# A decoder block on one core: per-engine call lists written out in place of a table of ticks

## The chip, the core and the metric

One core of a Trainium2 chip runs the whole program in one launch. The metric is the device time of one execution in microseconds (us). The kernel before has a median of 279.81 us over 3 runs (279.69 to 280.71). One further execution was profiled; it took 280.03 us, of which 278.30 us lie between its first and last instruction (the span). All positions below are us from the start of that span.

## The reference, cut to what matters

Three pre-LayerNorm blocks, each added to x (8 batches of 128 tokens, 256 wide):

```python
def _L0_attn_ref(x, Wq, Wk, Wv, Wo):        # 16 heads of 16
    scores = jnp.einsum('bthd,bshd->bhts', q, k)
    scores = scores * jnp.tril(jnp.ones((T, T)))      # masked scores are 0, not -inf
    attn = jax.nn.softmax(scores / T ** 0.5, axis=-1)
    out = jnp.einsum('bhts,bshd->bthd', attn, v).reshape(B, T, H * Dh)
    return out @ Wo
def _L0_xattn_ref(k, v, q, ssm_kernel, D, head_dim):   # k = v = ctx_2048, 16 heads of 8 x 8 products
    kv = jnp.einsum('bhil,bhjl->bijhl', k_, v_)
    y = irfft(rfft(kv, 2L) * rfft(ssm_kernel, 2L))[..., :L]     # a causal convolution over 256
    out = jnp.einsum('bijhl,bhil->bjhl', y + kv * D, q_)
def _L0_ffn_ref(x, ...):                    # 4-bit codes times block scales, 256 -> 2048 -> 256
    inter = gelu(x @ Wg.T) * (x @ Wu.T)
    return inter @ Wd.T
x = x + _L0_attn_ref(_layernorm(x), ...)
x = x + _L0_xattn_ref(ctx_2048, ctx_2048, _layernorm(x), ssm_kernel, D, 8)
x = x + _L0_ffn_ref(_layernorm(x), ...)
```

## The kernel before

The program is written engine by engine: one in-order instruction list each for TensorE, VectorE, ScalarE, GpSimd and SyncE, joined by semaphores. An instruction that waits holds everything behind it in its engine's list. There are three parts in time.

Up to about 28.7 us: x is normalised and transposed, split into a high and a low half-precision part, and projected to q, k and v. q and k go through a scratch tensor in DRAM (L347, L355) to be packed into the tile QK, in two groups of four batches.

Then the middle, until unit 8 of the MLP. `convolve(h, lc)` (L1024 on) does the causal convolution of one head in three matmuls; each result is copied out of psum by `conv_out` on ScalarE, and the factors are formed by `products(h)` on VectorE and on GpSimd in a ring of four. The first CONV_EARLY = 9 heads use the four psum banks 2 to 5 and run ahead of everything else, the others use banks 6 and 7. For each batch b the attention then goes: `scores(b, p)` on TensorE; `pair_max` (L816) and `max_pieces` (L832 to L836) on VectorE; a transpose of the maxima (L1186); `mT` (L685) on ScalarE; two small DMAs into rows of QK, issued by SyncE (`max_rows`, L363); `scores_t(b, p)` (L1092), which waits for those rows; exp (`probs`, L596); `attend` (L1108); `pv_out`; a transpose (L1209) and the sum over later tokens (L1213); `normalise` (L842 to L851) on VectorE; a transpose of the heads (L1219); the output projection with the residual (L1163, L1165); X is copied back (L712). Then LayerNorm 2 (statistics on VectorE L725, eps on ScalarE L643, power on GpSimd L403, apply on ScalarE L651), the transposed query (L1196), `conv_products` on GpSimd (L476 and L479, one call per half), their sum (`sum_slots`, L886) on VectorE, the add (L1177, L1179), LayerNorm 3 and the transposed MLP input (L1203), split by ScalarE (L698) and VectorE (L925).

The MLP is 32 units: `gate_and_up(u)` (L980, 12 matmuls), gelu (L635) and `act_hi` (L625) on ScalarE, `gate_up` (L894) on VectorE, `act_lo` (L500) on GpSimd, `down(u)` (L1150, 12 matmuls). Units 0 to 7 need only batches 0 to 3 and run between the last batches of the middle; unit 8 is the first that needs all eight. The 4-bit weights are decoded per step j: a DMA of codes and scales (`load_codes`, L301 to L306), four integer operations on VectorE (`codes_split`, `codes_join`, L859 to L871), two products on GpSimd (`decode_scale`, L492), the high part on ScalarE (`w_hi_step`, L618) and the low part on VectorE (`w_lo`, L876). ScalarE also issues the code loads of steps 1 to 3 behind its w_hi_step.

The order of the middle comes from a table: every kind of call has a tick (T_SCORES = 0, T_ST = 4, T_QT = 10, T_YT = 15 and so on), a batch every two ticks, UNIT_TICKS for the eight early units, DECODE for the four early steps. Each engine's part has one loop `for t in range(TICKS)` that runs through the kinds in one fixed order in every tick:

```python
(T_SCORES, T_SPLIT, T_MPT, T_ST, T_ATT, T_PVOUT, T_TOK, T_NORM, T_OT, T_PROJ, T_LN2, T_RSTD2, T_APPLY2,
 T_QT, T_MIX, T_MIX2, T_SUM, T_SUM2, T_RT, T_LN3, T_RSTD3, T_APPLY3, T_YT) = (
    0, 1, 3, 4, 5, 6, 7, 7, 8, 9, 8, 9, 9, 10, 11, 12, 12, 12, 13, 13, 14, 15, 15)
CONV_EARLY = 9
CONV_RATE = 2
UNIT_TICKS = (22, 23, 24, 24, 25, 26, 28, 29)
DECODE = (1, 5, 19, 23)
```

Psum banks 6 and 7 are handed from call to call: `take(n, reader, count)` makes TensorE wait for the reader of the call that used the bank last in its list, so a new order also makes new pairs.

Behind the middle stands a plain loop over units 8 to 31 on each engine, then the residual add and the output DMAs.

Of the kernel before, what the change touches and what calls it, by code (L numbers as in the profile page):

```python
# [37 lines left out]

def build(nc, x_d, ctx_d, wqkv_d, wo_d, ker_d, skip_d, gu_scale_d, down_scale_d, codes_d, out_d):  # L50
# [4 lines left out]
    with ctx:  # L55
# [9 lines left out]

# [37 lines left out]
        def bits2(j):  # L103
# [62 lines left out]

# [49 lines left out]

        (T_SCORES, T_SPLIT, T_MPT, T_ST, T_ATT, T_PVOUT, T_TOK, T_NORM, T_OT, T_PROJ, T_LN2, T_RSTD2, T_APPLY2,  # L230
         T_QT, T_MIX, T_MIX2, T_SUM, T_SUM2, T_RT, T_LN3, T_RSTD3, T_APPLY3, T_YT) = (
            0, 1, 3, 4, 5, 6, 7, 7, 8, 9, 8, 9, 9, 10, 11, 12, 12, 12, 13, 13, 14, 15, 15)
# [10 lines left out]
        TICKS = max(2 * (B - 1) + T_YT, UNIT_TICKS[-1],  # L243
                    DECODE[EARLY - 1] + 3) + 1

# [5 lines left out]
        def early_units(t):  # L251

            return [u for u, tick in enumerate(UNIT_TICKS) if tick == t]

        def early_decode(t, at):

            return [j for j in range(EARLY) if DECODE[j] + at == t]

# [4 lines left out]

        def batch(t, at):

            b, r = divmod(t - at, 2)
            return [b] if r == 0 and 0 <= b < B else []

        def pair_of_groups(t, at):

            n = t - at
            return [divmod(n, 2)] if 0 <= n < 2 * B else []

        def group(t, at):

            return [(b, 2 * p + par) for b, p in pair_of_groups(t, at) for par in range(2)]

        def conv_heads(t):

            return [h for h in range(CONV_EARLY + CONV_RATE * t, CONV_EARLY + CONV_RATE * (t + 1)) if h < H]  # L280

# [94 lines left out]
        def _(pool):  # L376
# [124 lines left out]

            for h in range(KVR, CONV_EARLY + CONV_RATE):
                products(h)
            for t in range(TICKS):
                for b in batch(t, T_MIX2):
                    conv_products(b, 1)
                for b in batch(t, T_RSTD3):
                    pool.wait_ge(s_veps[2], b + 1)
                    rstds(2, b, 1)
                for j in early_decode(t, 2):  # L510
                    decode_scale(j, 1)
                for h in conv_heads(t + 1):
                    if h >= KVR:
                        products(h)
                for b in batch(t, T_MIX):
                    conv_products(b, 0)
                for b in batch(t, T_RSTD2):
                    pool.wait_ge(s_veps[1], b + 1)
                    rstds(1, b, 1)
                for j in early_decode(t, 1):  # L520
                    decode_scale(j, 0)
                for u in early_units(t):
                    if u >= 1:
                        act_lo(u - 1)
# [7 lines left out]
        def _(sc):  # L532
# [94 lines left out]
            def unit(u):  # L627
# [9 lines left out]
                if u >= 1:  # L637
                    act_hi(u - 1)
# [15 lines left out]
            for h in range(CONV_EARLY):  # L654
                for lc in range(2):
                    conv_out(h, lc)
            for t in range(TICKS):
                for b in batch(t, T_QT):
                    sc.wait_ge(s_qt, b + 1)
                    if b >= 2:  # L660
                        sc.wait_ge(s_z, 4 * (b - 2) + 4)
                    s_.activation(view(qx[:, b % 2], [[16, 2 * H], [1, HD]], 4),
# [10 lines left out]
                for b in batch(t, T_RSTD3):  # L673
                    ln_eps(2, b)
# [615 lines left out]
```

## Time and profile before

| what | value |
|---|---|
| median of 3 runs | 279.81 us (279.69 to 280.71) |
| profiled execution | 280.03 us, span 278.30 us |
| TensorE busy | 250.9 us, 90% of the span |
| VectorE, ScalarE, GpSimd busy | 162.5, 129.9, 149.3 us |
| mean granted TensorE clock | 0.972 |
| first convolution matmul | 28.66 us |
| first gate matmul of unit 0 | 138.96 us |
| first gate matmul of unit 8 | 177.50 us |
| last down matmul ends | 272.60 us |

In the rows PE is TensorE's matmuls, PEld its weight loads, DVE VectorE, ACT ScalarE, POOL GpSimd, SP SyncE; a q behind the name is the engine's own sequencer or the DMAs that it issues. L and a number is a line of the kernel. Busy shares average over parts with different limits, so the stages are to be read singly.

### The profile page before, as it was taken

To read this page: it belongs to the slowest core of one execution; us is meant where nothing else is said; L and a number is where in the kernel's file an instruction comes from. 1 tells how busy PE (TensorE), PEld (TensorE's weight loads), DVE (VectorE), ACT (ScalarE), POOL (GpSimd) and SP (SyncE) were. 2 spreads that over 40 slices of the span, in tenths; PEclk is the share of its full clock that TensorE was granted. 3 is DMA by queue.
4 is the path that set the end of the run, shared out by engine and by line. 5 is a ranking of instruction groups with operands and counts; after the bars stand their busy time and mean duration, and the time that the engine had idled before them with its cause. 6 is when DMAs were issued, how large, how long until landed. Compare 5 with 4: busy or idle time off the path is not lost.

```text
span 278.3 us, 5004 instructions
## 1 busy us (share of the span) xinstructions
PE 250.9 (90%) x1872; PEld 161.9 (58%) x1872; DVE 162.5 (58%) x280; ACT 129.9 (47%) x281; POOL 149.3 (54%) x172
## 2 busy tenths in 40 slices
PE   7999999965999887895598998999999999999993
PEld 7765775533665655673454655556665566556662
DVE  2888523989786999668658364251725446131114
ACT  2454665545466666764555254331435243432230
POOL 3278464413116596759988995228354554723330
PEclk9999999999799999978979999999999999999998
DMA  6998969130300000000420030000303000000004
GB/s 200 389 318 199 181 224 173 30 114 4 117 1 4 2 1 6 1 2 0 124 102 2 0 115 0 1 4 0 113 2 113 3 2 0 0 2 0 0 2 151
DMA packets 15104, 18.81 MB, mean 68 GB/s; under 512 B 1448, under 2 KB 12776, under 8 KB 15080
## 3 DMA queue, kind: packets, MB, share of 16 engines
q1 hardware_dynamic: 13832, 16.13, 21.4%
q10 hardware_dynamic: 1248, 2.36, 2.7%
q8 instruction: 15, 0.25, 0.4%
q14 instruction: 9, 0.07, 0.1%
HBM read 15.21 MB, written 3.15 MB: 66 GB/s over the span
## 4 chain that ended last, share of the span: by engine, by line
PE 56%; DVE 5%; POOL 4%; issue 3%; ACT 2%; DVEq 0%; POOLq 0%; ACTq 0%
PE bank L980 30%; PE bank L1150 15%; PE bank L1165 2%; PE bank L1163 2%; POOL w L492 1%; PE bank L1177 1%; DVE o_sb L851 1%; POOL arena L476 1%; PE bank L1179 1%; PE bank L1108 1%; DVE XN L946 1%; ACT XN L651 1%; POOL rstd L403 1%; POOL arena L479 1%; PE bank L1203 1%
## 5 line engine op out<-in xcount | busy, mean ns | idle before, releaser
L500 POOL TENSOR_TENSOR QK<-QK 128x512 f16<-128x512 f32 x31 | 35.9, 1160 | 56.0 <-ACT QK L625 56.0
L894 DVE SCALAR_TENSOR_TENSOR QK<-bank,QK 128x512 f32<-128x512 f32 x32 | 22.0, 689 | 61.2 <-PE bank L980 61.2
L635 ACT ACTIVATE QK<-bank 128x512 f32<-128x512 f32 x32 | 19.1, 597 | 70.5 <-PE bank L980 70.3
L980 PE MATMUL bank<-xTh,Wa 128*128 128x512 f16 x128 | 41.9, 389 | 0.0
L980 PE MATMUL bank<-xTh,Wb 128*128 128x512 f16 x128 | 40.7, 379 | 0.0
L476 POOL TENSOR_TENSOR arena<-Ys,qx 128x640 f32<-128x640 f32 x16 | 25.1, 1568 | 2.0 <-ACT qx L665 2.0
L980 PE MATMUL bank<-xTl,Wa 128*128 128x512 f16 x64 | 25.0, 391 | 0.0
L980 PE MATMUL bank<-xTl,Wb 128*128 128x512 f16 x64 | 24.3, 379 | 0.0
L816 DVE TENSOR_REDUCE mx<-bank 128x8 f32<-128x1024 f32 x16 | 19.4, 1212 | 7.7 <-PE bank L1073 7.6
L1150 PE MATMUL bank<-Wa,QK 128*128 128x256 f16 x192 | 23.6, 273 | 0.0
L403 POOL TENSOR_TENSOR rstd<-veps,nhalf 128x1 f32<-128x1 f32 x16 | 9.6, 597 | 25.6 <-ACT veps L643 25.6
L1150 PE MATMUL bank<-Wb,QK 128*128 128x256 f16 x192 | 23.3, 273 | 0.0
L1150 PEld LDWEIGHTS bank<-Wa,QK 128*128 128x128 f16 x192 | 18.8, 98 | 5.6 <-POOL QK L500 0.2
L1150 PEld LDWEIGHTS bank<-Wb,QK 128*128 128x128 f16 x192 | 18.7, 98 | 5.3
L492 POOL TENSOR_TENSOR w<-arena 128x768 f32<-128x768 f16 x12 | 21.7, 1813 | 0.0
L725 DVE BATCH_NORM_STATS2 stats<-X 128x6 f32<-128x256 f32 x24 | 10.0, 417 | 19.0 <-ACT X L712 10.6
L980 PEld LDWEIGHTS bank<-xTh,Wa 128*128 128x128 f16 x128 | 12.8, 100 | 14.0 <-issue 1.3
L886 DVE TENSOR_REDUCE R<-arena 128x128 f32<-128x1024 f32 x16 | 18.9, 1207 | 2.7 <-POOL arena L479 2.7
L625 ACT ACTIVATE QK<-QK 128x512 f16<-128x512 f32 x32 | 19.9, 622 | 1.0 <-DVE QK L894 1.0
L980 PEld LDWEIGHTS bank<-xTh,Wb 128*128 128x128 f16 x128 | 12.5, 98 | 13.4
L446 POOL TENSOR_TENSOR arena<-arena 128x320 f32<-128x320 f32 x16 | 13.7, 865 | 12.0 <-PE bank L1038 12.0
L479 POOL TENSOR_TENSOR arena<-Ys,qx 128x384 f32<-128x384 f32 x16 | 20.1, 1256 | 0.0
(145 smaller groups left out, 509.8 us busy)
## 6 DMA issues: line engine op xcount, KB each, us to landing
arena<-in_ker SPq DMA_DIRECT2D x2, 1024.0 KB, 12.0
QK<-qk_scratch SPq DMA_DIRECT2D x8, 256.0 KB, 5.9
arena<-in_ctx SPq DMA_DIRECT2D x2, 768.0 KB, 7.8
qk_scratch<-Wa SPq DMA_DIRECT2D x12, 128.0 KB, 3.4
arena<-in_codes SPq DMA_DIRECT2D x4, 384.0 KB
QK<-qk_scratch SPq DMA_DIRECT2D x8, 128.0 KB, 5.8
arena<-in_gu_scale SPq DMA_DIRECT2D x4, 256.0 KB
out<-XN SPq DMA_DIRECT2D x4, 256.0 KB, 2.4
```

Source lines behind the costliest of these rows:

```text
L446: g_.tensor_tensor(view(KV[:, h % KVR, m, :], [[40, B], [8, NPAIR], [1, HD]]), view(a, [[12 * H, B], [0, NPAIR], [1, HD]]), view(a, [[12 * ...
L476: g_.tensor_tensor(view(Z[:, r], [[64, H], [1, NPAIR], [NSLOT, HD]], rows), view(Ys[:, 0, 0], [every, [DIAG, NPAIR], [1, HD]], convolved), ...
L479: g_.tensor_tensor(view(Z[:, r], [[64, H], [1, 3], [NSLOT, HD]], rows + NPAIR), view(Ys[:, 0, 0], [every, [DIAG - 1, 3], [1, HD]], convolv ...
L492: g_.tensor_tensor(W32[:, nib, :], view(bits(j).bitcast(F16), [[2, 768]], nib), scales(j), ALU.mult).then_inc(s_w32, 1)
L500: g_.tensor_tensor(il[:, u % IR], val[:, u % VR], ih[:, u % IR], ALU.subtract).then_inc(s_il, 1)
L625: s_.activation(ih[:, u % IR], val[:, u % VR], ACT.Copy).then_inc(s_ih, 1)
L635: s_.activation(val[:, u % VR], bank[2 * (u % 2)][:, :], ACT.Gelu_apprx_tanh, scale=1.0 / W_GAIN).then_inc(s_gel, 1)
L816: v_.tensor_reduce(mx[:, b % 2, 8 * p:8 * p + 8], psum[:, 0:2, :].rearrange("p g (h t) -> p (g h) t", h=4), AX.X, ALU.max).then_inc(s_max, 1)
L886: v_.tensor_reduce(R[:, b % 2, H * half:H * half + H], view(Z[:, b % 2], [[NSLOT, H * HD], [1, NSLOT]], 1024 * half), AX.X, ALU.add).then_ ...
L894: v_.scalar_tensor_tensor(out=val[:, u % VR], in0=bank[2 * (u % 2) + 1][:, :], scalar=UP_SCALE, in1=val[:, u % VR], op0=ALU.mult, op1=ALU. ...
L980: ins = mmul(out, a(c), w(c), start=(n == 0), stop=(n == 3 * len(chunks) - 1))
L1150: last = mmul(out, a[:, u % IR, t], w[j % RW][:, nib, 512:768], start=((j, nib) == (0, 0) and tt % 2 == 0 and n == 0), stop=((j, nib) == ( ...
```

## The change

The tick table, its helper functions and the five loops over ticks are gone. Each engine's part now has small named functions (one kind of call each, with the waits that the loop body had) and a list of single calls written out one under the other. Every operation stays on its engine, with its operands and its waits; the lists order them anew, in no regular pattern. CONV_EARLY is 13, so heads 0 to 12 use psum banks 2 to 5 and the first `scores_t` waits for the copies of 13 heads. The convolutions are no longer ahead of everything: `row_scores(0, 0)` stands behind head 3. VectorE's products(h), formerly ahead of the ticks up to head 10, are mixed into the list. ScalarE's `unit(u)`, which did gelu(u) and act_hi(u - 1) together, is split into two calls. SyncE's list is as before. The loop over units 8 to 31 is as before. The diff, cut to its core (renamed helpers keep their bodies):

```diff
-        (T_SCORES, T_SPLIT, T_MPT, T_ST, T_ATT, T_PVOUT, T_TOK, T_NORM, T_OT, T_PROJ, T_LN2, T_RSTD2, T_APPLY2,
...
-        CONV_EARLY = 9
-        CONV_RATE = 2
+        CONV_EARLY = 13
-        UNIT_TICKS = (22, 23, 24, 24, 25, 26, 28, 29)
-        EARLY = len(UNIT_TICKS) // 2
-        DECODE = (1, 5, 19, 23)
+        EARLY = 4
...
 GpSimd
+            products(8)
+            decode_scale(0, 0)
+            products(9)
+            products(10)
+            decode_scale(0, 1)
...
+            decode_scale(1, 0)
+            decode_scale(1, 1)
+            decode_scale(2, 0)
+            rstd_cross(0)
+            decode_scale(2, 1)
+            conv_products(0, 0)
+            conv_products(0, 1)
+            rstd_cross(1)
+            rstd_cross(2)
...
+            conv_products(5, 1)
+            rstd_ffn(4)
+            decode_scale(3, 0)
+            rstd_cross(7)
+            decode_scale(3, 1)
+            act_lo(0)
+            rstd_ffn(5)
+            act_lo(1)
+            conv_products(6, 0)
+            conv_products(6, 1)
+            conv_products(7, 0)
+            act_lo(2)
+            conv_products(7, 1)
...
 ScalarE
+            def decode_hi(j):
+                w_hi_step(j)
+                if j + 1 < EARLY:
+                    load_codes(sc, j + 1)
...
+            conv_out(8, 0)
+            decode_hi(0)
+            conv_out(8, 1)
+            conv_out(9, 0)
+            take_max(0)
...
+            pv_out(0)
+            take_max(1)
+            decode_hi(1)
+            probs(1, 0)
...
 VectorE
+            products(4)
+            products(5)
+            products(6)
+            decode_codes(0)
+            pair_max(0, 0)
+            products(7)
...
+            ffn_lo(1)
+            w_lo(2)
+            sum_slots(3, 1)
+            ffn_lo(2)
+            normalise(6)
+            stats_cross(5)
+            stats_ffn(3)
+            sum_slots(4, 0)
+            sum_slots(4, 1)
+            stats_cross(6)
+            normalise(7)
...
 TensorE
-            for h in range(CONV_EARLY):
-                for lc in range(2):
-                    convolve(h, lc)
...
+            convolve(3, 1)
+            row_scores(0, 0)
+            convolve(4, 0)
...
+            convolve(6, 1)
+            row_scores(0, 1)
+            convolve(7, 0)
...
+            row_scores(2, 1)
+            key_scores(0, 0)
+            convolve(14, 0)
+            convolve(14, 1)
+            key_scores(0, 1)
+            convolve(15, 0)
+            attend(0, 0)
+            row_scores(3, 0)
+            convolve(15, 1)
...
+            attend(7, 3)
+            project_out(5)
+            add_cross(3)
+            turn_heads(6)
+            turn_values(7)
+            project_out(6)
+            turn_ffn(3)
+            turn_query(5)
+            add_cross(4)
+            turn_heads(7)
+            gate_and_up(0)
+            turn_query(6)
+            project_out(7)
+            gate_and_up(1)
+            turn_ffn(4)
+            add_cross(5)
+            gate_and_up(2)
+            gate_and_up(3)
+            down(0)
+            down(1)
+            turn_ffn(5)
+            turn_query(7)
+            gate_and_up(4)
+            gate_and_up(5)
+            add_cross(6)
+            gate_and_up(6)
+            down(2)
+            gate_and_up(7)
+            turn_ffn(6)
+            add_cross(7)
+            down(3)
+            down(4)
+            down(5)
+            turn_ffn(7)
             for u in range(2 * EARLY, UNITS):
                 gate_and_up(u)
                 down(u - 2)
```

## Rows read from the trace of the kernel before

**Rows 1.** The page's chain of work that ended last: share of the span by engine.
```profile
PE 56%; DVE 5%; POOL 4%; issue 3%; ACT 2%; DVEq 0%; POOLq 0%; ACTq 0%
```
**Rows 2.** Busy time by stage: stretch, length, busy per engine (count), clock, DMA share, GB/s.
```profile
28.66:43.29 14.63, 14.63 (x57) 10.07 (x56) 4.69 (x11) 9.95 (x35) 7.62 (x8) 1.00 0.89 207
43.29:83.80 40.51, 33.42 (x383) 21.30 (x382) 33.35 (x51) 21.93 (x55) 11.42 (x11) 0.96 0.31 68
83.80:139.00 55.20, 43.61 (x467) 30.57 (x468) 43.53 (x80) 33.53 (x77) 41.92 (x45) 0.94 0.07 18
139.00:177.50 38.50, 35.99 (x205) 21.78 (x202) 21.16 (x31) 18.80 (x40) 30.35 (x29) 0.96 0.12 40
177.50:272.60 95.10, 95.10 (x592) 57.62 (x590) 35.85 (x46) 32.89 (x53) 41.98 (x32) 1.00 0.06 18
```
**Rows 3.** The chain in order of time, late loop: start, us, what.
```profile
263.46 2.59 PE bank L980 x12
266.05 1.31 PE bank L1150 x12
```
**Rows 4.** The same chain in the middle, around the calls of three batches.
```profile
89.64 1.38 DVE o_sb L851
...
91.15 0.41 PE bank L1219 x2
91.56 0.56 PE bank L1108 x16
92.12 0.67 PE bank L1163 x2
92.79 0.86 PE bank L1165 x4
93.66 0.33 PE bank L1056 x4
93.98 0.23 PE bank L1073 x8
...
94.49 0.67 PE bank L1177 x2
95.16 0.44 PE bank L1179 x4
95.61 0.16 PE bank L1186
...
96.32 0.59 PE bank L1209 x4
96.91 0.47 PE bank L1213 x2
```
**Rows 5.** TensorE's waits from 28 to 178: who for whom, total, times, longest.
```profile
PE bank L1196 <- ACT XN L651: 5.9, 6, 2.7
PE bank L1056 <- DMA QK<-mT: 4.2, 5, 2.3
```
**Rows 6.** Single lines: ns min/median/max, first and last start; L816 from the page's groups.
```profile
L816 DVE TENSOR_REDUCE mx<-bank 128x8 f32<-128x1024 f32 x16 | 19.4, 1212 | 7.7 <-PE bank L1073 7.6
...
L851 DVE TENSOR_TENSOR o_sb<-num,rec x8: 424/1126/1720, 74.8 to 137.1; 128x256 f32<-128x256 f32 x8
...
L476 POOL TENSOR_TENSOR arena<-Ys,qx x16: 1554/1570/1577, 83.8 to 162.9; 128x640 f32<-128x640 f32 x16
...
L479 POOL TENSOR_TENSOR arena<-Ys,qx x16: 999/1024/2512, 85.3 to 164.4; 128x384 f32<-128x384 f32 x16
```
**Rows 7.** GpSimd in order of time beside the first row of Rows 4.
```profile
89.15 1.58 POOL L476 TENSOR_TENSOR arena<-Ys,qx 128x640 f32<-128x640 f32 x1
```
**Rows 8.** SyncE's issues (codes; packing of group 1) and VectorE's first decode, by time.
```profile
28.13 0.60 SPq L301 DMA_DIRECT2D XN<-in_codes  x1
...
39.67 5.10 SPq L355 DMA_DIRECT2D QK<-qk_scratch  x8
...
50.28 0.55 DVE L859 TENSOR_SCALAR xTl<-XN 128x768 int32<-128x768 int32 x1
```

More of the change, by code:

```diff
@@ L500, in act_lo, with rstd_cross @@
                 g_.tensor_tensor(il[:, u % IR], val[:, u % VR], ih[:, u % IR], ALU.subtract).then_inc(s_il, 1)
[L502 to L524, printed above, removed]
+            def rstd_cross(b):
+                pool.wait_ge(s_veps[1], b + 1)
+                rstds(1, b, 1)
@@ new lines, in _ @@
+            take_out(7)
+            ln_apply(2, 4)
+            gate_gelu(1)
+            ln_eps(1, 7)
+            take_ffn(4)
+            act_hi(0)
+            take_cross(5)
+            act_hi(1)
+            gate_gelu(2)
+            ln_apply(1, 7)
+            ln_eps(2, 5)
+            act_hi(2)
+            gate_gelu(3)
+            ln_apply(2, 5)
+            decode_hi(3)
+            act_hi(3)
+            take_query(7)
+            take_ffn(5)
+            gate_gelu(4)
+            act_hi(4)
@@ new lines, in turn_heads, with turn_max @@
+            def turn_heads(b):
+                take(7, s_ott, b + 1)
+                pe.wait_ge(s_och, 4 * b + 4)
+                for c in range(2):
+                    last = t_.transpose(bank[7][:, P * c:P * c + P], o_sb[:, b % 2, P * c:P * c + P],
+                                        ident[:, :])
+                last.then_inc(s_ot, 1)
+            def turn_max(b):
+                take(7, s_mt, b + 1)
+                pe.wait_ge(s_mch, b + 1)
+                mmul(bank[7][0:2 * H, 0:P], mp[:, b % 2, :], identh[:, :], start=True, stop=True).then_inc(s_mpt, 1)
@@ new lines, in _ @@
+            project_out(3)
+            key_scores(4, 1)
+            row_scores(7, 0)
+            attend(4, 0)
+            turn_max(6)
+            attend(4, 1)
+            key_scores(5, 0)
+            attend(4, 2)
+            attend(4, 3)
+            key_scores(5, 1)
+            turn_values(4)
+            attend(5, 0)
+            key_scores(6, 0)
+            row_scores(7, 1)
+            turn_ffn(0)
+            attend(5, 1)
+            add_cross(1)
+            turn_heads(4)
+            key_scores(6, 1)
@@ new lines, in _ @@
+            attend(5, 2)
+            project_out(4)
+            turn_query(3)
+            attend(5, 3)
+            attend(6, 0)
+            attend(6, 1)
+            add_cross(2)
+            attend(6, 2)
+            attend(6, 3)
+            turn_max(7)
+            turn_values(5)
+            turn_ffn(1)
+            turn_query(4)
+            key_scores(7, 0)
+            turn_values(6)
+            turn_heads(5)
+            key_scores(7, 1)
+            turn_ffn(2)
+            attend(7, 0)
```

608 lines of the change are left out of this document (423 added, 185 removed).

## The prediction

> **What bounds the kernel now.** I read the chain of work that ended last first. Its shares by engine [rows 1] give TensorE 56%; followed in time, the chain is one unbroken run of TensorE from 173.76 us on: each further unit of the MLP is 2.59 us of gate and up matmuls and 1.31 us of down matmuls [rows 3], with nothing between. From 177.50 to 272.60 TensorE is busy 95.10 of 95.10 us at full granted clock (last row of [rows 2]). That loop (units 8 to 31 and the last two downs) isn't touched by the change, and what follows it (residual add, output) isn't either. So the whole question is when unit 8 starts; everything behind it is a constant. The other end of the stretch is fixed too: up to 28.66 us (LayerNorm 1, projections) no call list is touched. What the change can move is the stretch from 28.66 to 177.50, 148.8 us.
>
> In that stretch I read the busy time by stage [rows 2]. TensorE is idle 0 us, then 40.51 - 33.42 = 7.1, then 55.20 - 43.61 = 11.6, then 38.50 - 35.99 = 2.5: 21.2 us in all. The granted clock is below 1 in the last three: 0.96, 0.94 and 0.96 of stretches of 40.5, 55.2 and 38.5 us, which is 1.6 + 3.3 + 1.5 = 6.4 us of TensorE time lost at the lower level of 1.2 GHz. In the same rows VectorE has 33.35 of 40.51 and 43.53 of 55.20 us: in these two it is as loaded as TensorE, which matters below. The waits say what ended the idle time [rows 5]: TensorE stood for LayerNorm's result from ScalarE (5.9 us in 6 waits) and for the row maxima that travel by DMA (4.2 us in 5 waits). These are latencies of a chain that goes TensorE, VectorE, ScalarE, GpSimd and back, cut by in-order queues. A better order can hide them.
>
> **The work that stays.** No operation is added, removed or given to another engine; only the order in each queue changes. So I count what TensorE must issue between 28.66 and unit 8. Convolutions: nine heads fill the 14.63 us of the first stretch [rows 2], so sixteen take 26.0. From the chain's pieces [rows 4]: row scores 0.33 + 0.23 = 0.56, the key scores the same, 32 in all, 17.6 (I take 0.55); attention with V 0.56 per two groups, 16 times, 9.0; output projection 0.67 + 0.86 = 1.53, 8 times, 12.2; adding the cross block 0.67 + 0.44 where TensorE isn't packed and less where it is, I take 0.95, 7.6; turning the values 0.59 + 0.47 = 1.06, 8.5; turning the heads 0.41, 3.3, and the query and MLP input about the same, 6.1; the maxima 0.16, 1.3. Eight gate and up at 2.59 and six down at 1.31 [rows 3]: 20.7 + 7.9. The sum is 120.2 us. Check: 120.2 + 21.2 idle + 6.4 clock = 147.8 of 148.8; 1.0 us is left over and I carry it.
>
> **What is moved.** I followed the four new call lists by hand beside each other, each call at the duration of its rows, each wait as written.
>
> Convolutions. Nine heads ran ahead of any attention, then two per tick; now row scores (0,0) come after four heads, and thirteen heads use the four banks of psum 2 to 5. Row scores need the packed scratch DMAs of group 0. SyncE has issued them by about 28.1, just before the codes [rows 8], and I take them as landed by 35.1, when head 3 ends (TensorE waits at most 1 us if not). VectorE decodes the codes of step 0 ahead of the row maximum (0,0), after products(6), and not at 50.28 [rows 8] but from about 37.5, when I take the codes as landed: four operations, 2.9 us. Behind that wait on VectorE's queue stand the maximum (0,0), products(7) and, through them, TensorE's row scores (0,1) and head 7. I get 1.1 us of TensorE idle there. ScalarE's decode_hi(0), with its wait for both decode_scale(0) and its three DMA issues, now stands ahead of conv_out(8,1); behind it waits convolve(10,1), which needs that bank. It costs nothing as long as head 10 is reached after about 48.6, which is so in my walk by about 0.5 us. In return, at 60 to 61 us two more row scores, both key scores of batch 0 and an attention group are already issued. Thirteen heads in banks 2 to 5 make the first key scores wait for conv_out(12,1), about 54.7, which is 1.5 us ahead of its need. Row scores (3,0), issued at 65.1 before, end at 60.4.
>
> Attention. Per batch TensorE has some 8 us and VectorE has four reduces of 1.21 [rows 6] (maxima, and sums over as many elements), and by my reading of its shorter calls some 3.7 more, about 8.5. My walk puts single waits of 0.3 to 1.2 us: for the mT rows before key scores (1,0), which now come after the ScalarE decode_hi(1) with its DMA issues; for exp before (1,1); for XN and take_query around 87 to 91; for take_ffn and the last mT rows at 109 to 111. The first product of the cross block on GpSimd starts at about 79.3 and not 83.80 (first start of L476 [rows 6]), as project_out(0) comes at 69.6. The last attend ends near 115.7; before, it ended near 130.9.
>
> Tail. After the last attend TensorE still has about 42 us of work, and the chain of the last batch (values, normalise, heads, projection, statistics, query, 5.2 us of products on GpSimd, sum, statistics, MLP input, low part) is about 21.6 us long. So units 0 to 7 cover it if they start early. The first, gate_and_up(0), starts at 125.5 in my walk (139.0 before), the last products end on GpSimd near 150.2 (164.4 + 2.5 = 166.9 before [rows 6]). At the end stands a wait the old order did not have: turn_ffn(7) is TensorE's last call before unit 8, and ffn_lo(7) follows it; 0.9 to 1.2 us (before, unit 7 and down(5) lay between). GpSimd's act_lo and decode_scale(3) are moved past the cross products; SyncE's list is as it was, and its code loads for steps 4 to 7 depend on earlier events than before.
>
> **The sum.** In the walk unit 8 starts at 161.6, 132.9 us after 28.66; the calls as the walk costs them (projections at 1.46, the shorter of two patterns) are 118.9 of these, so its waits are 14.0 us. The walk has no low clock. The clock fell before behind the thin stretch at 60 to 70 and again between 118 and 144; fewer idle gaps should leave about half, 3.0 us (bounds 0 and 6.4). So 120.2 + 1.0 + 14.0 + 3.0 = 138.2 us in place of 148.8: -10.6 us. On the profiled execution's 280.03 us (its span 278.30, rest 1.73) this is 269.4 us. That execution is 0.2 above the median of the runs, 279.81, which changes nothing.
>
> **A rule weighed.** normalise's last operation takes between 0.42 and 1.72 us [rows 6]. One of 1.38 starts at 89.64 [rows 4] while a product of GpSimd runs from 89.15 to 90.73 [rows 7], and ends 0.3 us behind it, the time that a short one needs. The Trainium skill (SBUF — State Buffer, "Who interferes with whom") says that a VectorE instruction with two SBUF inputs contends with a GpSimd instruction that reads SBUF and fully blocks if it comes second; the trace agrees. It speaks against this change, as a denser GpSimd blocks more VectorE work. In rows of this case: my walk has normalise at 1.6 us, unblocked. Before, the median was 1.13, some 0.7 us of loss in each; if all eight are blocked at the longest, 1.72 - 0.42 = 1.3 us each, it is 10.4 us of VectorE. I expect most of it beside TensorE's other work; rival F is the case that it isn't.
>
> **Rivals.**
> A, forecast: 269.4.
> B, GpSimd's own queue keeps its pace. Its sixteen cross products took from 83.8 to 166.9, 83.1 us, for 16 x (1.57 + 1.02) = 41 us of work at the medians [rows 6]. If blocked VectorE work and ScalarE's queue stretch them again to 83.1 from 79.3, they end at 162.4 and unit 8 comes 10.6 us later as before, at 173.0: -4.5, 275.5. For it: VectorE is as full as TensorE up to 139. Against: the gaps were waits for veps and qx, which now come earlier.
> C, denser than my walk: no low clock and 11 us of waits: 120.2 + 1.0 + 11 = 132.2, -16.6, 263.4. For it: TensorE's work allows it, and GpSimd's floor (79.3 + 41, about 20 for rstds, decodes and low parts between, and 6.5 for the chain behind the last product) is 147. Against: I have left every blocked operation out.
> D, slower: the codes of step 0 land late. decode_codes(0) holds VectorE's queue from 35.6 and TensorE's heads 7 to 15 behind it. Issued at 28.13 while the DMA engines are full (share 0.89 to 43.3 [rows 2]), they are only known to be there at 50.28. If they land then, all behind slips by 50.28 - 37.5 = 12.8 us: -10.6 + 12.8 = +2.2, 282.2. It decides from a landing at about 48. Against: SyncE's wait for scratch writes issued after the codes ended at 39.67 [rows 8].
> E, nothing: the new waits eat the old ones, 279.8.
> F, every o_sb operation (L851) is blocked behind a GpSimd product and all of it is on the path: -10.6 + 10.4 = -0.2 us, 279.8 too. For it: VectorE's load up to 139; against: TensorE has other calls queued before most turn_heads.
>
> **How the numbers follow.** A 0.52, B 0.17, C 0.15, D 0.10, E 0.03, F 0.03. Predicted 269.4. The range leaves D, E and F out and the far ends of C and B: 263.0 to 277.0. Beyond 0.5% (1.4 us, what a measurement of this kernel can tell from none) faster: A, B, C, 0.84; within: E and F, 0.06; slower: 0.10.
>
> **What would show it.** Right: unit 8 at 165 to 169 with the loop behind it at 95.1 us as before; TensorE idle between 28.66 and there 13 to 16 us; last attend near 116; the first gate matmul near 126 to 130; L476 first at about 79. Wrong: VectorE's L859 waiting for a DMA past 42 with TensorE idle behind it (D); L479's last end past 160 and L851's mean above 1.3 us (B); a granted clock under 0.9 over the units 0 to 7, which would double their 28.6 us in part.

## The result

Twenty runs of the changed kernel have a median of 282.8 us (279.9 to 285.43), twenty of the kernel before beside them 279.94: the ratio is 1.0088, with a 95% interval of 1.0058 to 1.0119. It is slower by 0.9%, where 3.7% faster was forecast (269.4), and lies above the range. The profiled execution of the changed kernel took 281.73 us, span 280.0, mean granted clock 0.966.

| | before | forecast | after |
|---|---|---|---|
| first GpSimd cross product | 83.80 | 79.3 | 93.8 |
| last attend ends | 130.9 | 115.7 | 132.6 |
| unit 0 starts | 138.96 | 125.5 | 143.21 |
| unit 8 starts | 177.50 | 166.9 | 179.20 |
| TensorE idle from 28.66 to unit 8 | 21.2 | 15.0 | 22.6 |
| lost to the lower clock there | 6.4 | 3.0 | 8.4 |

The busy time by stage of the changed kernel, columns as in [rows 2]: the convolutions, the first batches, the middle up to unit 0, units 0 to 7, the late loop.

```profile
28.66:43.29 14.63, 12.58 (x64) 8.46 (x64) 6.75 (x13) 8.34 (x29) 5.63 (x6) 1.00 0.91 210
43.29:83.80 40.51, 33.02 (x285) 21.06 (x283) 31.50 (x44) 18.73 (x51) 14.06 (x12) 0.87 0.33 71
83.80:143.21 59.41, 47.29 (x565) 33.35 (x560) 51.34 (x85) 37.75 (x84) 39.79 (x45) 0.96 0.09 29
143.21:179.20 35.99, 35.05 (x205) 21.71 (x204) 23.43 (x33) 19.57 (x41) 30.76 (x30) 0.98 0.08 23
179.20:274.30 95.10, 95.10 (x590) 57.62 (x591) 35.84 (x45) 32.89 (x53) 42.04 (x32) 1.00 0.06 18
```

The late loop is the constant it was taken for: 95.10 us, TensorE full, clock 1.00. The idle time is 150.54 us less 127.95 of busy TensorE, 22.6 us; only 0.9 of it is left in units 0 to 7, as forecast. The clock column costs 40.51 x 0.13 + 59.41 x 0.04 + 35.99 x 0.02 = 8.4 us. VectorE has 51.34 of the 59.41 us up to unit 0. TensorE's waits from 28 to 180 us, us in total, times, longest:

```profile
PE bank L1268 <- DVE mx L943: 5.1, 4, 2.5
PE bank L1268 <- DMA QK<-mT: 3.6, 2, 3.0
PE bank L1399 <- DVE o_sb L978: 2.8, 2, 2.4
...
PE bank L1196 <- DVE xTl L1037: 0.9, 1, 0.9
```

TensorE's 5.9 us of waits for LayerNorm's result ahead of turn_query [rows 5] are gone, as meant; 1.2 us of such waits are left ahead of turn_ffn. In their place TensorE waits four times, 5.1 us, for the row maximum (L943), which VectorE's own queue holds up (before it was one wait of 2.5 us), and one wait for the maxima that travel by DMA is now 3.0 us.

Following the chain of work that ended last through the front shows how the first of these goes (start us, us, what; L986 and L900 from VectorE's order of time first):

```profile
39.18 0.56 DVE L986 TENSOR_SCALAR xTl<-XN 128x768 int32<-128x768 int32 x1 [4.92 <-DMA XN<-in_down_scale]
...
42.84 5.04 DVE L900 TENSOR_TENSOR arena<-arena 128x320 f32<-128x320 f32 x4
```
```profile
41.71 1.22 DVE mx L943
42.93 0.76 DVE arena L900
...
43.95 3.94 DVE arena L900 x3
47.89 1.14 DVE mx L943
49.03 0.05 issue
49.08 0.39 PE bank L1268 x4
```

VectorE stood 4.92 us for the codes of step 0, decoded them, and only at 41.71 took the maximum of row scores that had long been there. products(7) to (10) behind it took 5.04 us for four where a single one takes 0.49, beside GpSimd's reads; the longest of the sixteen products operations took 2.09 us here and 1.03 in the kernel before. Row scores (0,1) waited 1.99 us, (1,0) 2.52 us, and from 49 to 52 us TensorE's matmuls ran at the lower clock level.

The second place in the chain is at key scores (1,0):

```profile
70.76 0.60 SPq L299
71.36 0.04 issue
71.40 3.89 DMA QK<-mT
75.30 0.05 issue
75.34 0.40 PE bank L1268 x4
```

ScalarE's order of time at that place says what else was under way:

```profile
70.47 0.27 ACT L657 ACTIVATE mT<-bank 32x128 f16<-32x128 f32 x1
70.56 0.34 ACTq L237 DMA_DIRECT2D arena<-in_codes  x1
```

The rows' two transfers of 4 KB were handed over by SyncE from 70.76 us on, 0.2 us behind the first of the three loads (384 of 768 KB) with which decode_hi(1) fetches the codes of step 2; the other two followed at 70.92 and 71.57. From its hand-over to its landing the second transfer took 3.89 us. Key scores (1,0) themselves still ran at the upper level; behind a further wait of 1.12 us for exp, from 77.1 to 83.3 us, TensorE ran at the lower one.

### The profile page after: what moved, and what is told of

Its sections match the earlier page's. It is cut to its first block, busy times and chain, and to the rows that moved or that the text cites. A ratio compares the mean times of both kernels' runs of the same rounds, so it can differ in the third digit from the quotient of the medians.

```text
span 280.0 us, 5004 instructions
## 1 busy us (share of the span) xinstructions
PE 250.8 (90%) x1872; PEld 162.0 (58%) x1872; DVE 172.8 (62%) x280; ACT 130.1 (46%) x281; POOL 148.3 (53%) x172
## 4 chain that ended last, share of the span: by engine, by line
PE 75%; DVE 15%; DMA 3%; issue 2%; ACT 2%; POOL 1%; SPq 1%; DVEq 0%; POOLq 0%
PE bank L1196 36%; PE bank L1362 15%; PE bank L1268 3%; PE bank L1252 3%; PE bank L1254 3%; DVE mx L943 3%; PE bank L1250 2%; DVE arena L900 2%; PE bank L1436 2%; DVE o_sb L978 2%; DMA X<-in_x 2%; PE bank L1320 1%; DMA QK<-mT 1%; PE bank L1387 1%; PE bank L1304 1%
## 5 line engine op out<-in xcount | busy, mean ns | idle before, releaser
L1196 PE MATMUL bank<-xTh,Wa 128*128 128x512 f16 x128 | 41.2, 385 | 0.9 <-DVE xTl L1037 0.9
L412 POOL TENSOR_TENSOR arena<-Ys,qx 128x640 f32<-128x640 f32 x16 | 26.9, 1684 | 5.0 <-ACT qx L669 5.0
L558 ACT ACTIVATE Ys<-bank 128x320 f32<-128x320 f32 x32 | 14.5, 454 | 18.1 <-PE bank L1254 13.1
L943 DVE TENSOR_REDUCE mx<-bank 128x8 f32<-128x1024 f32 x16 | 19.5, 1216 | 3.2 <-PE bank L1285 3.2
L578 ACT ACTIVATE PT<-bank 128x1024 f32<-128x1024 f32 x16 | 16.4, 1027 | 10.3 <-PE bank L1304 10.0
L339 POOL TENSOR_TENSOR rstd<-veps,nhalf 128x1 f32<-128x1 f32 x16 | 8.8, 551 | 19.6 <-ACT veps L623 19.4
```

The source lines that it names most:

```text
L412: g_.tensor_tensor(view(Z[:, r], [[64, H], [1, NPAIR], [NSLOT, HD]], rows), view(Ys[:, 0, 0], [every, [DIAG, NPAIR], [1, HD]], convolved), ...
L558: s_.activation(view(Ys[:, h, lc], [[YROW, B], [DIAG, NPAIR], [1, HD]]), conv_bank(h, lc)[:, 0:320].rearrange("p (b d m) -> p b d m", b=B, ...
L578: s_.activation(PT[:, 2 * (n % 2):2 * (n % 2) + 2].rearrange("p g h t -> p g (h t)"), psum[:, 2:4, :], ACT.Exp, scale=SCALE).then_inc(s_ex ...
L943: v_.tensor_reduce(mx[:, b % 2, 8 * p:8 * p + 8], psum[:, 0:2, :].rearrange("p g (h t) -> p (g h) t", h=4), AX.X, ALU.max).then_inc(s_max, 1)
L1196: ins = mmul(out, a(c), w(c), start=(n == 0), stop=(n == 3 * len(chunks) - 1))
```

## The experiments

Ratios are to the kernel before, in the same set of runs. The changed kernel stands at 1.0088 (1.0058 to 1.0119) from its own set, so a difference to it carries both intervals. Positions are from one profiled execution of each kernel. They scatter: in the changed kernel, x1 and y1 below, whose calls are the same up to there, turn_max(0) starts at 54.69, 52.27 and 55.44 us.

**Which half of the order.** Two kernels take one half of the order from each side.

```diff
 g1: per engine
-(new list)
+(the calls of the old ticks 0 to 3, nine heads early), then the rest as in the new list
 g2: per engine
-(new list)
+(those same calls in the new order, thirteen heads early), then the rest as in the old list
```

> The changed kernel, but every engine first runs the calls of the old ticks 0 to 3 in the old order (nine heads ahead, CONV_EARLY 9, decode of step 0 late), then the rest in the new order. Theory FRONT (the loss is made in the first stretch: new row scores (1,0) came at 49.1 where my walk had 44.6, key scores (1,0) at 75.3 against 65.9): the rest of the new order is good, unit 8 starts near 170 to 173, 273 to 276 us. Theory PORTS (VectorE and GpSimd block each other more wherever the new order packs them): the middle keeps its loss, unit 8 at 177 to 180, 279 to 283 us.

> The reverse: the calls of the old ticks 0 to 3 in the new order (CONV_EARLY 13, row scores between the heads, step 0 decoded early), then all the rest in the old order. FRONT: as bad as or worse than the changed kernel, 283 to 287 us, since the front costs some 3 to 5 us and the old rest gains nothing. PORTS: near the kernel before, 279 to 282 us.

Measured: 1.0155 (1.0121 to 1.0189) and 1.014 (1.0057 to 1.0222). Both are slower than the kernel before, and neither is better than the changed one. g1 (284.04 us) lies above what either theory gave it, g2 (285.39) where FRONT put it. With the old front TensorE lost nothing up to 60 us (30.65 of 31.34 us busy, clock 1.00, as before), but from 60 to 100 the clock was 0.79. Neither half is the culprit by itself. I took that as a sign that the loss is in single places, which the runs below test.

**GpSimd's reads.** In both orders (p1 the new one, p2 the old), GpSimd's scale products and convolution products are replaced by memsets of the same tiles.

```diff
-g_.tensor_tensor(W32[:, nib, :], view(bits(j)...), scales(j), ALU.mult)
+own(g_.memset(W32[:, nib, :], 0.001))
+g_.memset(W32[:, nib, :], 0.001)
...
```

> The changed kernel with GpSimd's decode_scale and conv_products replaced by memsets of the same tiles and about the same length (two of 768 elements; two of 1024 and two of 512), so that GpSimd reads no SBUF in them: weights and cross products are constants, the output is not the reference's. PORTS: VectorE's busy time falls from 172.8 to about 155, o_sb is 0.42 us eight times, the products of head 7 to 10 take 2 us and not 5.0, unit 8 starts at 168 to 172, 271 to 275 us. If ports don't matter: VectorE's blocked operations overlap other waits and the time stays 280 to 283 us.

> The kernel before with the same replacement (the order written as lists, which is the old order call by call). PORTS: it gains less than the changed kernel does, 2 to 5 us, 275 to 278 us, so that the new order would be the faster one by some 3 us without the blocking. If it gains as much as the new order does, the blocking costs both alike and does not explain the difference.

Measured: new order 0.9898 (0.9825 to 0.9971), old order 0.9759 (0.9687 to 0.9832). By ratios that is 1.9% off the new and 2.4% off the old; the intervals do not tell these two apart. The new order gained less than the 271 to 275 us that PORTS gave it (279.22). GpSimd itself is about as busy with the memsets, 144.7 us in place of 148.3. VectorE's o_sb operation (its group over 28.66 to 180 us: line, shapes, count, busy us, mean ns) in the changed kernel, then with the memsets:

```profile
L978 DVE TENSOR_TENSOR o_sb<-num,rec 128x256 f32<-128x256 f32 x8 | 8.4, 1048 | 0.3
```
```profile
L976 DVE TENSOR_TENSOR o_sb<-num,rec 128x256 f32<-128x256 f32 x8 | 3.4, 429 | 0.3
```

products(7) to (10) take 2.74 us with the memsets in place of 5.04. So the blocking is real and worth some 5 us, but the old order pays it too. It explains a part of the forecast's miss, not why the new order is slower than the old.

**The load and the rows.** Two calls are moved; then each alone.

```diff
 ScalarE (x1, y1)
 take_max(1)
+take_max(2)
 decode_hi(1)
 probs(1, 0)
-take_max(2)
 VectorE (x1, y2)
-w_lo(1)
 pair_max(4, 0)
+w_lo(1)
```

> The new lists with two calls moved: on ScalarE take_max(2) stands directly behind take_max(1), so that the transfer of its rows is handed over before the 768 KB load of weight codes that decode_hi(1) sends off; on VectorE w_lo(1) stands behind pair_max(4,0). Theory QUEUE (key_scores(1,0) waited 3.03 us for rows that landed 3.89 us after their issue, beside the code load): it begins about 1.4 us earlier or more against the rows' issue, the half clock of 77 to 83 us goes, and the kernel is 3 to 4 us faster than the changed one (about 279). Theory ORDER (the slip is spread over every place where VectorE is late, no one load makes it): the end moves by under 1 us.

> One half of the two-call edit alone: ScalarE's take_max(2) directly behind take_max(1), so that the transfer of its rows is handed over before the code load of decode_hi(1) is sent off. Two calls moved gave a ratio of 0.9927 where the changed kernel has 1.0088, and key_scores(1,0) then waited 0.88 us for rows where it had waited 3.03. Theory QUEUE (the rows behind the 768 KB load are the cause): this edit alone brings most of it, ratio .993 to .997, rows landing within 2.3 us of their issue, and the half clock of 77 to 83 us is gone. Theory W_LO (the 1.75 us of w_lo(1) ahead of pair_max(4,0) on VectorE are what counts): this edit alone leaves 1.003 or more.

> The other half alone: VectorE's w_lo(1) behind pair_max(4,0). Theory QUEUE: no more than 1 us faster than the changed kernel, ratio 1.004 to 1.009, the rows of key_scores(1,0) still land 3.5 us or more after their issue. Theory W_LO: ratio .993 to .999.

Measured: both 0.9927 (0.9888 to 0.9967); ScalarE's call alone 0.9924 (0.9885 to 0.9963); VectorE's alone 1.0067 (1.0004 to 1.0131). The one call on ScalarE turns 0.9% slower into 0.8% faster, 4.6 us, and the other does nothing that can be told. The chain in the kernel with that one call moved:

```profile
72.15 1.75 DMA QK<-mT
```

The same transfer takes 1.75 us where it took 3.89, key scores (1,0) start 2.44 us after the hand-over (4.58 in the changed kernel), and the clock over 60 to 100 us is 0.96 in place of 0.87. Theory QUEUE stands. The load is not absent in this kernel: it is handed over at 72.59 us, 0.44 us behind this transfer. The edit also hands over the rows of batch 2 earlier, at 72.81 and not 77.20, but key scores (2,0) waited for nothing in either kernel.

**The same in the old order (w3).**

```diff
 ScalarE, kernel before
+decode_hi(1)
 take_max(2)
 probs(1, 1)
-decode_hi(1)
```

> The kernel before with one call moved on ScalarE: decode_hi(1), which sends off the 768 KB load of the codes of step 2, directly ahead of take_max(2), whose rows key_scores(2,0) needs; it stood two calls behind. Theory QUEUE (rows handed over right behind a code load land 1.5 us or more later, in whatever order of calls): the rows of batch 2 land 3.5 us or more after their issue, the time goes up by 1 to 4 us, ratio 1.004 to 1.014. Theory NEW ORDER ONLY (the old order has its rows two calls ahead of use and hides it): ratio within .003 of 1.

Measured: 1.0052 (1.0007 to 1.0098). The rows of batch 2 were handed over at 74.27 us and key scores (2,0) started at 78.09, 3.82 us later, after a wait of 1.43 us that the kernel before does not have there. So the place of this call matters in the old order too, and the old one loses about 1.5 us by it. This run does not show that the transfer alone is the reason. take_max(2) now also stands behind w_hi_step and the load's issue on ScalarE: its operand was there at 72.4 us and it ran at 73.98, so the rows were handed over some 1.6 us late before any byte of them moved. That alone covers the wait of 1.43 us; the slower way from hand-over to start (3.82 us, 2.44 in y1) would cover 1.38. The clean evidence for QUEUE is y1, where take_max(1), which hands over the rows of batch 1, kept its place.

**The decode earlier or later.** In the first kernel the decode of steps 0 to 2 stands as late as before on all engines; in the second, one call moved as above, w_lo(1) as in x1, and only step 0 later.

```diff
 VectorE (y3)
-decode_codes(0)
 pair_max(0, 0)
 ...
 max_pieces(0)
+decode_codes(0)
 ...
 products(15)
+w_lo(0)
 ScalarE (y3)
 conv_out(13, 1)
+decode_hi(0)
```

> The new lists, but the weight decode of steps 0 to 2 (codes, scale products, high and low halves, with the code loads that they send off) stands as late among the other calls as in the kernel before. Theory EARLY DECODE (some 9 us of decode put ahead of the first batches' maxima and of conv products on VectorE and ScalarE is what made row_scores(0,1), (1,0) and key_scores(1,0) wait, and each wait was followed by a stretch at half clock): the waits of 1.99 and 2.52 us at 41 to 49 us fall under 1 us each, unit 0 starts 4 to 6 us earlier than 143.2, and the end comes at 276 to 278. Theory ORDER (VectorE is the bound from 100 us on wherever the decode stands): the decode comes back later, unit 0 stays within 1.5 us of 143.2.

> The two calls moved, and the decode of step 0 moved later by itself: its codes on VectorE behind max_pieces(0) (they stood ahead of pair_max(0,0)), the low half behind products(15), its two scale products on GpSimd behind products(12) and (14), the high half on ScalarE behind conv_out(13,1). Steps 1 and 2 stay early. With all three late the third turn_max began 6 us earlier than in the changed kernel and unit 0 8 us later. Theory FRONT WAIT (the 4.92 us that VectorE waits for the codes of step 0 and the 3.6 us of scale products beside products(7) to (10) are lost for good): unit 0 at 132 to 134 against 136.6 with two calls moved, ratio about .98. Theory SHIFT (what step 0's decode does not cost at 36 to 48 us it costs at 50 to 60, where VectorE has as much to do; and the later load of the next codes makes step 1 late): ratio within .005 of .9927, unit 0 136 to 138.

Measured: 1.0315 (1.0248 to 1.0382) and 1.0116 (0.9994 to 1.0238). Both misses for the theories that made the early decode guilty. With all three late, turn_max(0) came at 48.40 us in place of 54.69, and unit 0 at 151.39 in place of 143.21: more was lost behind the front than it gained. In the second, VectorE's w_lo(0) waited 4.75 us for a high half that stood far back on ScalarE, so that kernel carries a fault of its own and says little of step 0. To have all three late is worse; the best place of each was open.

**Ahead of the codes.** Only two VectorE calls are taken out from behind the wait for the codes, with ScalarE's call moved as well and without.

```diff
 VectorE (v1; w2 with take_max(2) moved too)
+pair_max(0, 0)
+products(7)
 decode_codes(0)
-pair_max(0, 0)
-products(7)
```

> The changed kernel with take_max(2) behind take_max(1), and on VectorE pair_max(0,0) and products(7) ahead of decode_codes(0): VectorE stood 4.9 to 5.6 us waiting for the codes of step 0, which land at 39.2 to 39.9 us, while the maxima of row_scores(0,0), ready at 36.6 us, were queued behind it. Nothing else moves. Theory FRONT WAIT: row_scores(0,1) begins 1.5 to 2 us earlier than 42.98, and half or more of that arrives at unit 0: ratio .985 to .989 (one call moved gave .9924). Theory SHIFT (VectorE's work behind the codes begins when they land in either order, so pair_max(0,1) and row_scores(1,0) come no earlier): ratio .990 to .995.

> The changed kernel with one edit: on VectorE pair_max(0,0) and products(7) ahead of decode_codes(0); ScalarE's calls as in the changed kernel, so the rows of key_scores(1,0) still follow the code load. With both edits the ratio was 0.9858 and with the other alone 0.9924, in two sets, and their intervals touch. Theory FRONT WAIT (VectorE's wait for the codes is on the path by itself): ratio 1.000 to 1.004 where the changed kernel had 1.0088, row_scores(0,1) at 41.5 or earlier, unit 0 some 2 us earlier. Theory CHANCE (the difference of the two sets is scatter): 1.006 to 1.010.

Measured: with both 0.9858 (0.977 to 0.9947); alone 0.9959 (0.9928 to 0.999). Alone it is worth 1.3%, 3.6 us, more than its theory gave it (1.000 to 1.004). VectorE's first decode in it, and the transfer of the rows, which still follow the load:

```profile
38.39 0.56 DVE L986 TENSOR_SCALAR xTl<-XN 128x768 int32<-128x768 int32 x1 [0.91 <-DMA XN<-in_down_scale]
```
```profile
68.68 4.23 DMA QK<-mT
```

VectorE now waits 0.91 us for the codes and not 4.92, and TensorE's clock over 28.66 to 60 us is 1.00 in place of 0.95. Row scores (0,1) start at 40.79 without a wait (42.98 in the changed kernel), (1,0) at 45.54 in place of 49.08, turn_max(0) at 49.52 in place of 54.69. These positions flatter the edit: w2, with the same front, has turn_max(0) at 52.25 and a clock of 0.95 over 28.66 to 60, as without the edit. The ratio is the safer measure. A wait of 1.78 us ahead of (1,0) is left, since products(8) to (10) still take 3.43 us for three. The transfer behind the load takes 4.23 us: the two faults are separate.

**GpSimd's reads on top, and the issue of the load.** To the kernel with both edits, once the memsets are added (w4), once the load of step 1's codes goes to SyncE (w5).

```diff
 ScalarE, decode_hi(j)
-if j + 1 < EARLY:
+if 1 < j + 1 < EARLY:
     load_codes(sc, j + 1)
 SyncE
+load_codes(sp, 1)
 for b in range(B):
     max_rows(b)
```

> The kernel of the first run of this set, with GpSimd's scale products and convolution products replaced by memsets of the same tiles of about the same length (the output is constant there): GpSimd then reads nothing beside VectorE. The same replacement brought 3.6 us to the changed kernel and 5.8 to the one before. Theory PORTS (what is left of the miss is mostly VectorE's instructions blocked by GpSimd's reads, which the walk had priced at nothing): 3 to 5 us faster than the first run of this set, ratio .97 to .976. Theory DENSE (the blocked time was VectorE's slack here): under 2 us.

> The kernel of the first run of this set, and the load of the codes of step 1 is sent off by SyncE ahead of the batches' rows, and no more by ScalarE, where its issue took 4.9 to 5.2 us at 47.6 us and conv_out(8,1) came only at 54.3, 6.8 us behind the call ahead of it. Theory BLOCKED SCALAR (heads 10 to 12 wait for bank copies that stand behind the load on ScalarE, and the half clock of 49 to 52 us is part of it): turn_max(0) 2 us or more earlier than 54.7, ratio 1 to 2% below the first run of this set. Theory SLACK (TensorE has row scores to do and waits for VectorE in this stretch): within .003 of it.

Measured: 0.9706 (0.9623 to 0.9789) and 0.9847 (0.9782 to 0.9912). Against 0.9858 the memsets bring a further 1.5%, 4.3 us, as theory PORTS had it, though the two intervals touch. The load by SyncE brings nothing that can be told. It was to free ScalarE, which in the changed kernel is held like this:

```profile
47.57 4.86 ACTq L237 DMA_DIRECT2D XN<-in_codes  x1
52.47 1.18 ACTq L239 DMA_DIRECT2D XN<-in_gu_scale  x1
53.68 0.62 ACTq L242 DMA_DIRECT2D XN<-in_down_scale  x1
54.34 0.45 ACT L558 ACTIVATE Ys<-bank 128x320 f32<-128x320 f32 x1 [5.29 <-PE bank L1254]
```

An issue that takes 0.34 us at 70.56 takes 4.86 us here, while the DMA engines are 0.74 busy, and conv_out(8,1) comes 6.8 us after the call ahead of it. TensorE had other calls and waited for VectorE at the time, so in the changed kernel it cost nothing: SLACK. That does not hold once the waits ahead of it are shorter. convolve(10,1) needs the bank that conv_out(8,1) empties, and it waited for ScalarE in v1 and, with the memsets, in w4 (TensorE's order of time):

```profile
53.00 0.81 PE L1252 MATMUL bank<-arena 128*128 128x320 f32 x2 [2.25 <-ACT Ys L561]
```
```profile
55.22 1.43 PE L1250 MATMUL bank<-arena 128*128 128x320 f32 x2 [4.27 <-ACT Ys L559]
```

In w4 the matmuls behind this wait ran at the lower level up to 60 us. In w2, the kernel that the load's move was tried on, it was 0.56 us, so there was little to win. The memsets and the load by SyncE were not run together.

**The clock by itself.** 31 extra products of 128 columns, whose results nobody reads, in four of TensorE's waits: in the changed kernel, with the late decode, and with the two calls moved.

```diff
+keep_warm(7, 7)
 row_scores(0, 1)
+keep_warm(7, 9)
 row_scores(1, 0)
+keep_warm(5, 11)
 key_scores(1, 0)
+keep_warm(5, 4)
 key_scores(1, 1)
```

> The new lists with 31 extra TensorE products of 128x128 columns whose results nobody reads, put into the four waits: 7 ahead of row_scores(0,1), 9 ahead of row_scores(1,0), 11 ahead of key_scores(1,0), 4 ahead of key_scores(1,1). They take no time where TensorE waits anyway. Theory CLOCK (the waits cost twice, once themselves and again by the half clock of the stretch behind them): the granted clock over 28.66 to 60 and 60 to 100 us rises from .95 and .87 to .98 or more, unit 0 starts 3 to 5 us earlier than 143.2 and the end at 277 to 279. Theory ORDER (VectorE's chain is as long at either clock): the clock rises, but the time gained is waited out again before turn_max and the end moves by under 1 us.

> Both of the last two edits together: decode of steps 0 to 2 late, and the 31 extra products in the waits. Theory EARLY DECODE with CLOCK: the gains add, unit 0 at 135 to 138 us, the end at 273 to 276. Theory ORDER: as the changed kernel within 1.5 us, since VectorE, 94% busy from 100 us to unit 0, sets the start of unit 0.

> The two calls moved, and the 31 extra products in the four waits. Theory CLOCK (2 us of the changed kernel's loss are half clock that follows the waits at 41 to 49 us, the rest of the low clock went with the rows' late landing): clock over 28.66 to 60 and 60 to 100 us from .95 and .94 to .98 or more, ratio .986 to .990. Theory COVER (the extra products lie as often on the path as in the waits, now that these are shorter): ratio .992 to .996.

Measured: 1.0007 (0.9974 to 1.004), 1.0384 (1.0322 to 1.0446), 0.9975 (0.9922 to 1.0029). The clock rose as wanted (1.00 and 0.96 in the first, where the changed kernel has 0.95 and 0.87), and the time followed only there, by 2.2 us. On top of the late decode and of the two calls moved the extra products gave nothing that can be told (1.0315 and 0.9927 without them, the intervals overlap). At 72 to 83 us the low clock goes with the wait: take the wait away (y1) and it goes too, at no price. For the front this is not shown: the clock up to 60 us is 1.00 in v1 and v2 but 0.95 in w2 and w5, with the same two calls ahead of the codes.

**Everything that helped, together (v2).** take_max(2), w_lo(1), pair_max(0,0) with products(7), and the load by SyncE.

> The changed kernel with all edits that gained or were neutral: take_max(2) behind take_max(1) on ScalarE, w_lo(1) behind pair_max(4,0), pair_max(0,0) and products(7) ahead of decode_codes(0) on VectorE, the load of the codes of step 1 sent off by SyncE. Theory QUEUE with FRONT WAIT: ratio .982 to .988, unit 0 at 134 to 137, so a version that beats both kernels by over 1%. Theory CHANCE: .990 to .994, no better than the one call moved.

Measured: 275.32 us, ratio 0.9796 (0.9754 to 0.9839), faster than both kernels by 2.0 and 2.9%. Busy time up to unit 0, which starts at 135.36 us; columns as above:

```profile
28.66:60.00 31.34, 28.73 (x177) 19.18 (x175) 25.18 (x38) 18.47 (x62) 14.32 (x16) 1.00 0.80 161
60.00:100.00 40.00, 31.55 (x399) 20.79 (x398) 31.23 (x52) 23.20 (x51) 17.11 (x17) 0.96 0.13 42
100.00:135.36 35.36, 28.51 (x333) 20.39 (x332) 33.97 (x53) 23.56 (x54) 27.72 (x33) 0.98 0.08 24
```

and the same of the changed kernel:

```profile
28.66:60.00 31.34, 25.96 (x138) 17.04 (x137) 20.66 (x31) 15.90 (x54) 14.30 (x14) 0.95 0.77 163
60.00:100.00 40.00, 32.33 (x384) 20.86 (x383) 28.05 (x45) 20.70 (x43) 13.18 (x10) 0.87 0.13 41
100.00:143.21 43.21, 34.60 (x382) 24.97 (x382) 40.88 (x66) 28.21 (x67) 32.00 (x38) 0.98 0.07 20
```

By 60 us VectorE has done 4.5 us more and by 100 us 7.7, and that is what is missing from its last stage: 33.97 against 40.88 us. From 100 us on VectorE is 96% busy in the one and 95% in the other, more than any other engine. I read it as the bound there, so that VectorE time lost earlier, while the engine could have worked, moves unit 0; no run tests this by itself.

## Why the prediction was wrong

The frame held. The late loop is unchanged, the change acts between 28.66 us and unit 8, and the floor of 120.2 us with the measured idle time and clock loss gives 120.2 + 22.6 + 8.4 = 151.2 for 150.5 measured. The two terms that failed are the waits of the hand walk, 14.0 us (with 1.0 left over, 15.0, where 22.6 were measured), and the clock, 3.0 us (8.4). Together they are 13.0 us; the start of unit 8 is 12.3 off and the median 13.4.

- **"single waits of 0.3 to 1.2 us: for the mT rows before key scores (1,0), which now come after the ScalarE decode_hi(1) with its DMA issues"**. This is the step that failed hardest. I saw the three issues ahead of the rows and counted only ScalarE's time for them, not that their 768 KB would be on the DMA engines first. The wait was 3.03 us, with a stretch at the lower clock behind it. Moving one call gave back 4.6 us, and with it alone the kernel would have been 0.8% faster.
- **"I get 1.1 us of TensorE idle there"** (the codes of step 0, taken as landed at 37.5). They were there at 39.18. The queue behind the wait was named rightly, its price was not: waits of 1.99, 0.56 and 2.52 us, and the clock fell. Taking two calls out from behind it gave 3.6 us. Rival D had this mechanism and priced only the lateness, one for one from 37.5: at 39.18 that is 1.7 us, and the sign turned at 48. Moving the calls gave 3.6 us, a third of the forecast gain, because the whole wait of 4.92 us stood ahead of ready work, the part up to 37.5 too. The sign of being wrong set for D (L859, now L986, waiting past 42) was never reached.
- **"I expect most of it beside TensorE's other work"** (GpSimd's reads blocking VectorE). The memsets give back 4.3 us on the kernel with both edits, 5.3 on the changed one. o_sb's mean was 1.05 us, inside the band of [rows 6]. The loss I had not listed was in other operations: products(7) to (10), 5.04 us for four, and max_pieces, whose 0.23 us operation took up to 1.86 us (below). The walk had priced all of these unblocked; rival F named only o_sb.
- **"It costs nothing as long as head 10 is reached after about 48.6"** (ScalarE's decode_hi(0) ahead of conv_out(8,1)). The walk took the three issues as short and reached head 10 some 0.5 us behind that. conv_out(8,1) started at 54.34 in the changed kernel, since the first issue alone took 4.86 us. It cost nothing only because TensorE was already late; in v1 the wait was 2.25 us and in w4 4.27. That is luck, and a term the walk had at nothing.
- **"Fewer idle gaps should leave about half, 3.0 us"** of the clock loss. The idle time did not shrink (22.6 us, before 21.2). Long waits came right behind one another at 41 to 49 and 72 to 77 us, and in the second place the stretch at the lower level was 6 us long.
- **Rival B**, GpSimd's pace: its cross products ran from 93.8 to 170.1 us (last start of L415 169.1 and 1.03 of its own), 76.3 us, between my 70.9 and B's 83.1. They started 14.5 us later than walked, and that is most of the 17.6 us by which unit 8 came later than in the walk. So it is the front that failed more than the pace, which was 5.4 us off.
- **The tail** came as forecast: 0.9 us of wait for ffn_lo(7) ahead of unit 8, and 0.94 us of idle time in units 0 to 7 where 2.5 had been.

The three causes in order: both edits take the changed kernel from 1.0088 to 0.9858 (6.4 us, less than their 4.6 and 3.6 alone), the memsets to 0.9706 (4.3 us). The forecast was 0.963. The 2.2 us that are left are within these intervals; the wait of 4.27 us in w4 for conv_out(8,1) is a likely home for them, which no run tested. That the new order is slower than the old, and not merely less fast than forecast, is shown to hang on the first two: each edit alone brings the ratio below 1, with its whole interval.

## What to carry to other kernels

When a call list is reordered, follow each small transfer that an engine waits for and ask what was sent off in the microseconds ahead of it, by any queue: a large prefetch belongs behind the small urgent one, and the place of one call decided the sign here. A wait that heads an in-order queue costs all the ready work behind it; put that work ahead, above all on an engine that is full later. A hand walk that adds single durations finds the mechanisms but not their size where two engines are both near full, so its waits deserve a wide upper bound.

## What the runs showed of the hardware

- The same 4 KB transfer took 1.75 us when the load was issued 0.44 us behind it, and 3.89 and 4.23 us when the first of three loads, 768 KB in all, had been issued by another engine 0.84 us ahead of it (0.2 us ahead of the first of the rows' two transfers); two different issuing engines did not keep them apart.
- The issue of one 384 KB load took 0.34 us at 70.56, where the DMA engines were idle (share 0.00), and 3.29 us (w2) to 5.90 us (p1) around 47 us, where they were 0.74 busy in the changed kernel. It held ScalarE's compute calls behind it.
- GpSimd also held up VectorE operations with one small tensor input. VectorE's and GpSimd's order of time around one such place in the changed kernel:

```profile
64.94 0.75 DVE L959 TENSOR_SCALAR ms<-mx,guard 128x16 f32<-128x16 f32 x1
65.60 1.86 DVE L960 TENSOR_SCALAR mp<-mx,guard 128x16 f16<-128x16 f32 x1
```
```profile
63.85 3.58 POOL L428 TENSOR_TENSOR w<-xTh,XN 128x768 f32<-128x768 f16 x2 [4.62 <-DVE xTh L998]
```

L960's median is 0.23 us; it ended with GpSimd's second product, at 67.4 us. Memsets of the same tiles did not hold up o_sb, whose mean fell to 0.43 us with them, but they did hold up these operations. In p1 L957 (the same operation as L959) took 0.78 us where its usual is 0.23, and ended at 122.34, a memset of GpSimd at 122.31:

```profile
121.56 0.78 DVE L957 TENSOR_SCALAR ms<-mx,guard 128x16 f32<-128x16 f32 x1
```
```profile
121.36 0.95 POOL L413 MEMSET arena<- 128x1024 f32 x1
```

So the memset kernels take away a part of the blocking and not all of it. max_pieces is 0.6 us of work and took 2.7 us beside the two products; at 108.61 it took 3.1 us and TensorE waited 1.5 us for it ahead of turn_max(6).
